# A 32-batch graph-attention kernel: the hardware loop over pairs of batches written out, all waits for constants

## The chip, the cores and the metric

The kernel runs on one core of one Trainium2 chip. The metric is the device time of one execution in microseconds. Before the change the median of three runs is 1394.42 us (1394.37 to 1395.95).

## What is computed

The reference takes 32 batches of 256 rows by 384 features, with one 256 x 256 boolean adjacency matrix per batch, and applies two residual layers:

```python
h = jnp.maximum(_layernorm(x, axis=-1), 0.0)
x = x + _L0_gnn_ref(h, Wq, bq, Wk, bk, Wv, bv, Wf, bf, adj)      # 6 heads of 64, masked softmax attention
h = jnp.maximum(_layernorm(x, axis=-1), 0.0)
x = x + _L1_gnn_ref(h, adj, W, b, w_src, w_dst, H_w, H_b)        # 12 heads of 32, graph attention, ELU, gate
```

In the second layer the score of a pair of rows is a sum of a source term and a destination term through a leaky ReLU, masked, and put through a softmax; the result passes an ELU and is mixed with the input by a sigmoid gate. The batches don't depend on one another.

## The kernel before, in words

All weights are loaded once and kept as two 16-bit parts each (three products make one), so the steady work is per batch. A batch is 256 rows in two tiles of 128 partitions; two to five batches are in flight at a time. Work is cut in steps (LN_T0, Q, K, QK, PT0, PV0, ...), each of which has a part on one or more engines.

The order of the steps is written out by hand for each engine, in ORDERS (L72 to L105). An entry such as `B GATE 0` names a phase, a step and an index; LAG (L64) says how far the phase's batch lies behind the iteration's number, so one iteration does phase L of batch n+2, P of n+1, A of n, B of n-1, C of n-2. `walk` (L382) goes through the iterations -2 to NB+2. Iterations -2 to 3 and 30 to 34 are written out ("straight code" in what follows). Iterations 4 to 29 are a hardware loop: `eng.Fori(0, LOOP)` (L394) with LOOP = 13 turns and two iterations in its body. Each engine has a loop of its own, with its own branch at the end of the body; so there are 12 jumps back per engine, and the thirteenth branch falls through.

The engines meet through semaphores that only count up. Count and Jobs (L121, L162) work out the value that a wait needs. In straight code it is a constant. In the loop it is an expression of the loop's register (`_value`, L145), which register instructions on the waiting engine compute before the wait. Where a wait comes several to an instruction, `ready` (L357) moves the value to one of three registers ahead of time, and the functions then wait for `s_pool_const` to reach 8, which has long been so, before the wait itself. DMA addresses of x, adj and the output are indexed with the loop register on the SP queue (`of_batch`, L424).

The steps that the texts below speak of:

- PE: `to_rows` (L501, products that make rows: V, OUT0, HEADS, GATE), `to_columns` (L515, Q and K), `transpose_probs` (L574), `qk` (L550), `pv1` (L637), `ln_t0` and `ln_t1` (L489). One iteration of PE's order begins with `C PT1 9, A QK 0, B GATE 0` and ends with `B PT1 8, B PV1 1`.
- DVE: `leaky1` (L986 and L993, steps SCORES1). The order ends with `B SCORES1 9` and begins with `C SCORES1 10`, so the end of the body lies between these two.
- ACT: `exp1` (L755) and `pt1` (L763). The order ends with `B EXP1 9` and begins with `C PT1 8, C EXP1 10`.
- POOL: `norm1` (L1115) and `norm0` (L1099); SP: the loads of x and adj and the store.

`qk` for index 0 writes a PSUM bank that SCORES1 11 reads and writes, and so waits for it (L544).

Of the kernel before, what the change touches and what calls it, by code (L numbers as in the profile page):

```python
# [50 lines left out]
YB = 3  # L51
# [56 lines left out]
class Batch:  # L108


    def __init__(self, ref, reg=None):
        self.ref, self.reg = ref, reg

    def back(self, k):
        return Batch(self.ref - k, self.reg)

    def value(self):
        return self.ref if self.reg is None else self.reg * 2 + self.ref


class Count:  # L121


    def __init__(self, n_batch, engine, per_step, unit=1):
        self.order, self.per_step, self.unit, self.n = ORDERS[engine], per_step, unit, n_batch
        self.starts = {-2: 0}
        for it in range(-2, n_batch + 3):
            self.starts[it + 1] = self.starts[it] + sum(per_step[s] for ph, s, _ in self.order if self._on(ph, it, s))
        self.per = self.starts[5] - self.starts[4]

# [13 lines left out]

    def _value(self, batch, n):  # L145
        v = n * self.unit
        return v if batch.reg is None else batch.reg * (2 * self.per * self.unit) + v

    def before(self, batch, step, idx=0, less=0):

        return self._value(batch, self._ahead(batch, step, idx) - less)

# [4 lines left out]
    def after(self, batch, step, idx=0, k=None):  # L157

        return self._value(batch, self._ahead(batch, step, idx) + (self.per_step[step] if k is None else k))


class Jobs(Count):  # L162
# [3 lines left out]
    def __init__(self, n_batch):  # L166
        super().__init__(n_batch, "PE", JOBS)
        assert 2 * self.per % self.BANKS == 0

# [7 lines left out]
    def before(self, batch, step, idx=0):  # L177

        v = self._ahead(batch, step, idx) // self.BANKS
        return v if batch.reg is None else batch.reg * (2 * self.per // self.BANKS) + v  # L180

# [4 lines left out]
def build(nc, x, adj, w_all, bq, bk, bv, bf, gat_b, w_src, w_dst, gate_b, out):  # L186
    NB = x.shape[0]
    LOOP = (NB - 6) // 2
    assert NB % 2 == 0 and LOOP >= 1

# [5 lines left out]
    with ExitStack() as ctx:  # L196
# [159 lines left out]

        def ready(eng, value):  # L357

            if isinstance(value, int):
                return value
            if eng.engine not in count_regs:
                count_regs[eng.engine] = [eng.alloc_register(f"count{i}_{eng.engine.name}") for i in range(3)]
            regs = count_regs[eng.engine]
            regs.append(regs.pop(0))
            eng.reg_mov(regs[-1], value)
            return regs[-1]

        count_regs = {}  # L370

        def loaded(b):

            v = 16 * (b.ref // 2 + 1)
            return v if b.reg is None else b.reg * 16 + v

# [5 lines left out]
        def walk(eng, order, parts, after={}):  # L382


            def iteration(it, reg=None):
                for phase, step, idx in order:
                    b = Batch(it - LAG[phase], reg)
                    if step in parts and 0 <= b.ref < NB:
                        parts[step](b, b.ref % 2, idx)
            for n in range(-2, 4):  # L390
                iteration(n)
                if n in after:
                    after[n]()
            with eng.Fori(0, LOOP) as j:  # L394
                iteration(4, j)
                iteration(5, j)
            for n in range(NB - 2, NB + 3):
                iteration(n)

# [4 lines left out]
        def _(sp):  # L404
# [18 lines left out]

            def of_batch(view, b, rows):  # L424
                return view[b.value()] if b.reg is None else view[bass.ds(b.value(), 1)].rearrange(rows)

            def load_x(b, par, _):
                x_b = of_batch(x_v, b, "a p t h -> (a p) t h")
                if b.ref >= 2:
                    sp.wait_ge(s_norm0, n_norm0.after(b.back(2), "NORM0"))  # L430
                    sp.wait_ge(s_xc, n_xc.after(b.back(2), "RES_ROW"))
                sp.dma_start(xb[par][:], x_b).then_inc(s_x[par], 16)

            def load_adj(b, par, _):
                adj_b = of_batch(adj_v, b, "a p t m -> (a p) t m")
                if b.ref >= 2:
                    used = ready(sp, n_mask1.after(b.back(2), "MASK1"))
                    sp.wait_ge(s_pool_const, 8)
                    sp.wait_ge(s_mask1, used)
                sp.dma_start(adj_raw[par][:], adj_b).then_inc(s_adj[par], 16)  # L440

            def store(b, par, _):
                out_b = of_batch(out_v, b, "a p t h -> (a p) t h")
                sp.wait_ge(s_sum, n_sum.after(b, "OUT_SUM"))
# [7 lines left out]
        def _(pe):  # L452
# [166 lines left out]
            def dst_t(b, par, _):  # L619
                bank, made, taken, _ = job(b, "DST_T")  # L620
                parts, free = ready(pe, n_sd.after(b, "SCORE_SUM")), ready(pe, n_job.before(b, "DST_T"))
                pe.wait_ge(s_pool_const, 8)
                pe.wait_ge(s_sd, parts)
# [157 lines left out]
        def _(dve):  # L781
# [49 lines left out]
            def gate_bias():  # L831

                own(V.tensor_scalar(gate_b_row[:], gate_b_row[:], wscale[:, WG:WG + 1], XS, ALU.mult, ALU.mult))
                for k in range(3):
# [13 lines left out]
            def aggregate(b, k, step, idx=0):  # L848
                written = ready(dve, n_bn.after(b, step, idx))
                dve.wait_ge(s_pool_const, 8)  # L850
                dve.wait_ge(s_bn, written)
# [57 lines left out]
            def scores0(b, par, u):  # L909
                masks = ready(dve, n_mask0.after(b, "MASK0"))  # L910
                scores = ready(dve, n_qk.after(b, "QK", u // 2))
                used = ready(dve, n_e0.before(b, "EXP0", u, YB - 1))
                dve.wait_ge(s_pool_const, 8)
                if u == 0:
# [54 lines left out]
            def leaky1(b, par, u):  # L969
# [19 lines left out]
                for hh in range(2):  # L989
                    written = ready(dve, n_lk.after(b, "SCORES1", u, hh + 1))  # L990
                    dve.wait_ge(s_pool_const, 8)
                    dve.wait_ge(s_lk, written)
# [41 lines left out]
        def _(pool):  # L1034
# [24 lines left out]
            def make_mask0(b, par, _):  # L1059
                here = ready(pool, loaded(b))  # L1060
                read = ready(pool, n_y0.after(b.back(1), "SCORES0", 5)) if b.ref >= 1 else None
                pool.wait_ge(s_pool_const, 8)
                pool.wait_ge(s_adj[par], here)
# [4 lines left out]
            def make_mask1(b, par, _):  # L1068
                here = ready(pool, loaded(b))
                read = ready(pool, n_y1.after(b.back(1), "SCORES1", 11)) if b.ref >= 1 else None  # L1070
                pool.wait_ge(s_pool_const, 8)
                pool.wait_ge(s_adj[par], here)
# [4 lines left out]
            def make_rstd(k, step, sstep):  # L1077
                def part(b, par, _):

                    here = ready(pool, n_mv.after(b, sstep))  # L1080
                    pool.wait_ge(s_pool_const, 8)
                    pool.wait_ge(s_mv, here)
# [6 lines left out]
            def norm0(b, par, _):  # L1089
                here = ready(pool, n_rstd.after(b, "RSTD0"))  # L1090
                if b.ref >= 1:
                    _, made, _, value = job(b.back(1), "LN_T0", 1)
                    used = ready(pool, value)
                pool.wait_ge(s_pool_const, 8)
                pool.wait_ge(s_rstd, here)
# [7 lines left out]
            def norm1(b, par, _):  # L1103
                here = ready(pool, n_rstd.after(b, "RSTD1"))
                if b.ref >= 1:
                    _, made, _, value = job(b.back(1), "LN_T1", 1)
                    used = ready(pool, value)
                    kept = ready(pool, n_hskip.after(b.back(1), "SKIP_H"))
                pool.wait_ge(s_pool_const, 8)
                pool.wait_ge(s_rstd, here)  # L1110
# [8 lines left out]
            def normp0(b, par, u):  # L1119
                here = ready(pool, n_np0.after(b, "NORMP0", u))  # L1120
                pool.wait_ge(s_pool_const, 8)
                pool.wait_ge(s_rec0, here)
# [31 lines left out]
            def gates(b, par, _):  # L1154

                jobs_ = [job(b, "GATE", t) for t in range(NT)]
                tanh = [ready(pool, value) for _, _, _, value in jobs_]
                used = ready(pool, n_fin.after(b.back(2), "FINISH", 1)) if b.ref >= 2 else None
                pool.wait_ge(s_pool_const, 8)
                for (_, _, taken, _), value in zip(jobs_, tanh):  # L1160
# [68 lines left out]
```

## Time and profile before

| | |
|---|---|
| median of 3 runs | 1394.42 us |
| profiled execution, device time | 1395.05 us |
| its span | 1393.1 us |
| PE (TensorE matmul) busy | 93% of the span |
| ACT, DVE, POOL busy | 91%, 88%, 65% |
| mean granted TensorE clock | 0.978 |

The device time is 1.95 us more than the span: what lies before the first and after the last recorded instruction. A "pause" is idle time in front of an instruction; in a timeline it stands in square brackets, with the instruction that ended it. "Issue" is time in which an engine waits for nothing that the profile shows. PEld is the weight load of TensorE.

### The profile page before, as it was taken

The numbers are of one execution on the slowest core, as the hardware profiler recorded it, in microseconds if no ns is written. First come the engines' busy times: TensorE is split into PE (matmuls) and PEld (weight loads), VectorE is DVE, ScalarE is ACT, GpSimd is POOL, SyncE is SP. The second block draws the span as 40 slices with busy tenths as digits, with TensorE's granted clock in tenths as the row PEclk, the third lists the DMA queues.
The fourth block names the chain that finished last, engine by engine and source line by source line (L and its number), as shares of the span: only waits on it lengthen the run. The fifth ranks groups of instructions, "written<-read, shape, count | busy, mean of one in ns | idle before, by whom it ended". The sixth has DMA issues, their size and how long they took to land.

```text
span 1393.1 us, 39297 instructions
## 1 busy us (share of the span) xinstructions
PE 1302.0 (93%) x10502; PEld 908.3 (65%) x10502; DVE 1221.0 (88%) x4457; ACT 1261.6 (91%) x3731; POOL 904.1 (65%) x1106
## 2 busy tenths in 40 slices
PE   2889999999999999999999999999999999999974
PEld 1567667766666776666677676767667666666642
DVE  3569999989898998989899898999989899999875
ACT  4469999989999999999999999999999999999975
POOL 3357777657766666777766676766667676567743
PEclk8899999999999999999999999999999999999986
DMA  5000000000000000000000000000000000000000
GB/s 151 13 14 15 26 13 27 27 26 14 26 25 13 25 25 26 14 26 15 23 25 25 15 25 26 12 26 25 25 15 25 25 14 26 25 25 3 13 13 24
DMA packets 29845, 33.28 MB, mean 24 GB/s; under 512 B 10464, under 2 KB 29664, under 8 KB 29664
## 3 DMA queue, kind: packets, MB, share of 16 engines
q1 hardware_dynamic: 29664, 31.62, 7.4%
q14 instruction: 159, 1.30, 0.3%
q8 instruction: 22, 0.36, 0.1%
HBM read 19.03 MB, written 12.58 MB: 23 GB/s over the span
## 4 chain that ended last, share of the span: by engine, by line
PE 48%; issue 15%; ACT 15%; DVE 14%; POOL 3%; DVEq 2%; DMA 1%; ACTq 0%; SPq 0%; POOLq 0%
PE job L501 14%; PE pt L574 10%; PE unit L550 7%; PE job L637 5%; DVE unit L986 4%; ACT p L755 4%; PE job L515 4%; ACT p L712 3%; PE job L489 3%; DVE y L993 3%; PE job L592 2%; ACT o1m L773 1%; ACT c L724 1%; DVE bn L868 1%; POOL xn L1115 1%
## 5 line engine op out<-in xcount | busy, mean ns | idle before, releaser
L755 ACT ACTIVATE p<-y,min 128x256 f32<-128x256 f32 x768 | 394.5, 537 | 10.2 <-DVE min L993 10.1
L986 DVE SCALAR_TENSOR_TENSOR unit<-unit,s,dst 128x256 f32<-128x256 f32 x768 | 336.6, 484 | 37.8 <-ACT p L755 33.6
L574 PE MATMUL pt<-ident,p 128*128 128x128 f32 x2304 | 356.6, 280 | 9.4 <-ACT p L755 5.6
L574 PEld LDWEIGHTS pt<-ident,p 128*128 128x128 f32 x2304 | 266.0, 142 | 84.5 <-issue 45.3
L501 PE MATMUL job<-w,h 128*128 128x384 f16 x1728 | 303.9, 328 | 0.9 <-DVE h L884 0.6
L993 DVE CUSTOM_DVE_ANT_0 y<-unit,mask 128x256 f32<-128x256 f32 x768 | 291.6, 417 | 0.3 <-issue 0.2
L1124 POOL TENSOR_SCALAR p<-p,rec 128x256 f32<-128x256 f32 x384 | 188.3, 506 | 116.1 <-DVE rec L927 111.5
L501 PEld LDWEIGHTS job<-w,h 128*128 128x128 f16 x1728 | 167.2, 98 | 107.9 <-DVE h L884 5.6
L763 ACT ACTIVATE pT<-pt 128x512 f32<-128x512 f32 x384 | 230.2, 621 | 7.4 <-issue 6.6
L712 ACT ACTIVATE p<-y,min 128x256 f32<-128x256 f32 x384 | 191.0, 503 | 37.5 <-PE pt L574 24.6
L515 PE MATMUL job<-h,w 128*128 128x256 f16 x1728 | 216.6, 274 | 1.4 <-DVE h L884 1.4
L920 DVE CUSTOM_DVE_ANT_0 y<-unit,mask 128x256 f32<-128x256 f32 x384 | 146.4, 421 | 45.4 <-PE unit L550 42.9
L515 PEld LDWEIGHTS job<-h,w 128*128 128x128 f16 x1728 | 169.6, 99 | 21.7 <-issue 1.8
L755 ACT ACTIVATION_READ_ACCUMULATOR p<-y,min 128x1 f32 x768 | 175.8, 229 | 0.0
L1185 POOL TENSOR_TENSOR y<-y,xskip 128x768 f32<-128x768 f32 x32 | 58.1, 1816 | 174.1 <-DVE y L1024 174.1
L550 PE MATMUL unit<-kT,qT 64*128 64x256 f32 x768 | 111.2, 409 | 28.1 <-DVE unit L986 23.5
L719 ACT ACTIVATE pT<-pt 128x512 f32<-128x512 f32 x192 | 111.3, 600 | 12.2 <-PE pt L574 12.1
L743 ACT ACTIVATE dst<-unit 128x512 f32<-128x512 f32 x192 | 118.3, 617 | 2.6 <-PE unit L565 1.7
L501 PE MATMUL job<-w,c 128*128 128x384 f16 x576 | 104.2, 327 | 1.0 <-DVE c L932 1.0
L637 PE MATMUL job<-pT,hv 128*32 128x256 f32 x1536 | 103.7, 388 | 0.7 <-ACT pT L763 0.7
L550 PEld LDWEIGHTS unit<-kT,qT 64*128 64x128 f32 x768 | 67.3, 189 | 52.7 <-DVE unit L986 26.3
L592 PE MATMUL job<-pT,vv 128*64 128x256 f32 x768 | 99.5, 395 | 0.0
(109 smaller groups left out, 2234.0 us busy)
## 6 DMA issues: line engine op xcount, KB each, us to landing
xb<-in_x_dram SPq DMA_DIRECT2D x32, 384.0 KB, 3.3
out_dram<-y SPq DMA_DIRECT2D x32, 384.0 KB, 2.5
pT<-in_w_all_dram SPq DMA_DIRECT2D x4, 576.0 KB, 10.4
adj_raw<-in_adj_dram SPq DMA_DIRECT2D x32, 64.0 KB, 1.9
prod<-in_w_all_dram SPq DMA_DIRECT2D x1, 576.0 KB, 5.0
p<-in_w_all_dram SPq DMA_DIRECT2D x1, 576.0 KB, 11.0
out_row<-in_bf_dram SPq DMA_DIRECT2D x1, 192.0 KB, 4.1
gate_b_row<-in_gate_b_dram SPq DMA_DIRECT2D x1, 192.0 KB, 6.2
```

What stands on the lines that cost most here:

```text
L501: last = mm(bank[:, 0:H], rows[:, i, c, t * P:(t + 1) * P], w16[:, w, j, c, :], start=n == 0, stop=(c, i, j) == (NC - 1, *TERMS[-1]))
L515: last = mm(bank[:, 0:T], w16[:, w, i, c, p * P:(p + 1) * P], h16[0][:, j, c, :], start=n == 0, stop=n == 3 * NC - 1)
L550: last = mm(unit_ps[(2 * p + hh) % 3][:, qt * T:(qt + 1) * T], qT[par][r, p, qt * P:(qt + 1) * P], kT[par][r, p, :], start=True, stop=True)
L574: last = nc.tensor.transpose(pt_ps[u % 2][:, (2 * hh + kt) * P:(2 * hh + kt + 1) * P], probs[:, u % 3, hh, kt * P:(kt + 1) * P], ident[:])
L637: last = mm(bank[D1 * q:D1 * (q + 1), 0:T], hv[par][:, kt, h * D1:(h + 1) * D1], pT1[:, g % 2, q, kt, :], start=kt == 0, stop=kt == NT - 1 ...
L712: last = op(p0[:, u % 3, hh, :], y0[:, u % YB, hh, :], ACT.Exp, bias=min0[:, u, hh:hh + 1], scale=-1.0, accum_out=sum0[:, u, hh:hh + 1])
L755: last = op(p1[:, u % 3, hh, :], y1[:, u % YB, hh, :], ACT.Exp, bias=min1[:, u, hh:hh + 1], scale=-1.0, accum_out=sum1[:, t, h:h + 1])
L763: op(pT1[:, g % 2, q_:q_ + 2, :, t * P:(t + 1) * P], pt_ps[u % 2][:].rearrange("p (h k q) -> p h k q", h=2, k=NT), ACT.Copy).then_inc(s_pT, 1)
L920: last = V.tensor_tensor_reduce(y0[:, u % YB, qt, :], unit_ps[u % 3][:, qt * T:(qt + 1) * T], mask0[:, qt, :], 1.0, 3.0e38, ALU.add, ALU.m ...
L986: V.scalar_tensor_tensor(leaky[:, hh * T:(hh + 1) * T], bank[:, hh * T:(hh + 1) * T], s8[par][:, t, h:h + 1], dst5[:, c % 2, hh, :], ALU.a ...
L993: last = V.tensor_tensor_reduce(y1[:, u % YB, hh, :], leaky[:, hh * T:(hh + 1) * T], mask1[:, t, :], 1.0, 3.0e38, ALU.add, ALU.min, min1[: ...
L1124: last = G.tensor_scalar(p0[:, u % 3, hh, :], p0[:, u % 3, hh, :], rec0[:, u, hh:hh + 1], 1.0, ALU.mult, ALU.mult)
```

## The change

The loop is gone: `walk` writes out all iterations in the same order. A batch has no register, every count is a constant, `ready` and the extra waits for `s_pool_const` are gone (one stands in the bias code of DVE and one ahead of POOL's walk), and the SP queue's addresses are constants.

```diff
-            def iteration(it, reg=None):
+            for n in range(-2, NB + 3):
                 for phase, step, idx in order:
-                    b = Batch(it - LAG[phase], reg)
+                    b = Batch(n - LAG[phase])
                     if step in parts and 0 <= b.ref < NB:
                         parts[step](b, b.ref % 2, idx)
-            for n in range(-2, 4):
-                iteration(n)
                 if n in after:
                     after[n]()
-            with eng.Fori(0, LOOP) as j:
-                iteration(4, j)
-                iteration(5, j)
-            for n in range(NB - 2, NB + 3):
-                iteration(n)
...
-    def _value(self, batch, n):
-        v = n * self.unit
-        return v if batch.reg is None else batch.reg * (2 * self.per * self.unit) + v
-
     def before(self, batch, step, idx=0, less=0):
 
-        return self._value(batch, self._ahead(batch, step, idx) - less)
+        return (self._ahead(batch, step, idx) - less) * self.unit
...
-                x_b = of_batch(x_v, b, "a p t h -> (a p) t h")
+                x_b = x_v[b.ref]
...
             def dst_t(b, par, _):
                 bank, made, taken, _ = job(b, "DST_T")
-                parts, free = ready(pe, n_sd.after(b, "SCORE_SUM")), ready(pe, n_job.before(b, "DST_T"))
-                pe.wait_ge(s_pool_const, 8)
+                parts, free = n_sd.after(b, "SCORE_SUM"), n_job.before(b, "DST_T")
                 pe.wait_ge(s_sd, parts)
                 pe.wait_ge(taken, free)
...
             def gate_bias():
 
+                dve.wait_ge(s_pool_const, 8)
...
                 for hh in range(2):
-                    written = ready(dve, n_lk.after(b, "SCORES1", u, hh + 1))
-                    dve.wait_ge(s_pool_const, 8)
+                    written = n_lk.after(b, "SCORES1", u, hh + 1)
                     dve.wait_ge(s_lk, written)
...
+            pool.wait_ge(s_pool_const, 8)
             walk(pool, ORDERS["POOL"],
```

The other places where `ready` and the wait for `s_pool_const` stood (SCORES0, the aggregates, the masks, RSTD, NORM0, NORM1, NORMP0, GATES, LOAD_ADJ) are changed in the same way.

## Rows read from the trace of the kernel before

**Rows 1.** The page: the span, and PE's busy time.

```profile
span 1393.1 us, 39297 instructions
PE 1302.0 (93%) x10502; PEld 908.3 (65%) x10502; DVE 1221.0 (88%) x4457; ACT 1261.6 (91%) x3731; POOL 904.1 (65%) x1106
```

**Rows 2.** Chain that ended last, whole span: start us, us, what (its longest pieces).

```profile
153.73 2.99 PE job L501 x18
...
193.61 2.99 PE job L501 x18
233.66 2.99 PE job L501 x18
...
317.27 2.99 PE job L501 x18
...
399.45 2.99 PE job L501 x18
...
481.36 2.99 PE job L501 x18
...
1218.95 2.99 PE job L501 x18
...
1258.83 2.99 PE job L501 x18
...
1298.70 2.99 PE job L501 x18
```

**Rows 3.** The chain in 135 to 175 us, straight code: shares by line.

```profile
by line: PE job L501 29.7%; PE pt L574 21.8%; PE job L515 15.3%; PE unit L550 8.0%; PE job L637 7.5%; PE job L592 7.3%; PE unit L565 3.8%; PE job L489 3.6%; PE job L645 1.6%; PE job L497 1.1%; PE job L627 0.5%
```

**Rows 4.** Stretches of PE: start:end us, length, PE busy, PEclk, DMA, GB/s.

```profile
135.00:175.00 40.00, 40.00 (x331) 1.00 0.08 23
...
282.60:286.10 3.50, 3.50 (x15) 0.51 0.00 0
...
440.00:522.00 82.00, 79.97 (x659) 1.00 0.07 22
```

**Rows 5.** Timeline of all engines around the second jump back.

```profile
360.29 0.09 DVE L993 DVE_READ_ACCUMULATOR2_ANT min<- 128x1 f32 x1
...
362.31 0.56 ACT L755 ACTIVATE p<-y,min 128x256 f32<-128x256 f32 x1
...
363.38 0.88 DVE L986 SCALAR_TENSOR_TENSOR unit<-unit,s,dst 128x256 f32<-128x256 f32 x2 [3.01 <-ACT p L755]
363.68 0.60 ACT L763 ACTIVATE pT<-pt 128x512 f32<-128x512 f32 x1 [0.72 <-issue]
...
365.92 0.49 PE L550 MATMUL unit<-kT,qT 64*128 64x256 f32 x2 [2.17 <-DVE unit L986]
```

**Rows 6.** The chain in 358 to 367 us, around the same jump: two pieces.

```profile
360.37 2.70 issue
363.08 0.06 DVEq L394
```

**Rows 7.** Timeline of DVE where the thirteenth branch falls through.

```profile
1261.97 0.08 DVE L993 DVE_READ_ACCUMULATOR2_ANT min<- 128x1 f32 x1
1262.18 0.88 DVE L986 SCALAR_TENSOR_TENSOR unit<-unit,s,dst 128x256 f32<-128x256 f32 x2
```

**Rows 8.** Waits in 215 to 255 us (an even iteration of the loop).

```profile
PEld job L489 <- POOL xn L1115: 0.4, 1, 0.4
```

**Rows 9.** DMA queues in 90 to 265 us (packets, MB, share), and one issue.

```profile
q8 instruction: 12, 0.20, 0.5%
q14 instruction: 14, 0.11, 0.2%
...
xb<-in_x_dram SPq DMA_DIRECT2D x5, 384.0 KB, 3.5
```

**Rows 10.** DMA queues in 300 to 1262 us (the turns after the first), and one issue.

```profile
q1 hardware_dynamic: 19040, 19.99, 6.6%
q14 instruction: 126, 1.03, 0.3%
...
xb<-in_x_dram SPq DMA_DIRECT2D x23, 384.0 KB, 3.3
```

**Rows 11.** Whole span, the SP queue's waits: us, times, longest.

```profile
SPq L439 <- POOL mask L1075: 727.5, 30, 38.5
```

**Rows 12.** The page: the granted TensorE clock in 40 slices.

```profile
PEclk8899999999999999999999999999999999999986
```

More of the change, by code:

```diff
@@ L108, with __init__ @@
 class Batch:
-    def __init__(self, ref, reg=None):
-        self.ref, self.reg = ref, reg
+    def __init__(self, ref):
+        self.ref = ref
     def back(self, k):
-        return Batch(self.ref - k, self.reg)
-    def value(self):
-        return self.ref if self.reg is None else self.reg * 2 + self.ref
+        return Batch(self.ref - k)
 class Count:
@@ L128, in __init__ @@
             self.starts[it + 1] = self.starts[it] + sum(per_step[s] for ph, s, _ in self.order if self._on(ph, it, s))
-        self.per = self.starts[5] - self.starts[4]
     def _on(self, phase, it, step):
@@ L157, in after @@
     def after(self, batch, step, idx=0, k=None):
-        return self._value(batch, self._ahead(batch, step, idx) + (self.per_step[step] if k is None else k))
+        return (self._ahead(batch, step, idx) + (self.per_step[step] if k is None else k)) * self.unit
 class Jobs(Count):
@@ L167, in __init__ @@
         super().__init__(n_batch, "PE", JOBS)
-        assert 2 * self.per % self.BANKS == 0
     def bank(self, batch, step, idx):
@@ L177, in before @@
     def before(self, batch, step, idx=0):
-        v = self._ahead(batch, step, idx) // self.BANKS
-        return v if batch.reg is None else batch.reg * (2 * self.per // self.BANKS) + v
+        return self._ahead(batch, step, idx) // self.BANKS
     def after(self, batch, step, idx=0):
@@ L187, in build @@
     NB = x.shape[0]
-    LOOP = (NB - 6) // 2
-    assert NB % 2 == 0 and LOOP >= 1
     x_v = x.rearrange("b (t p) h -> b p t h", p=P)
@@ L355, in build @@
         s_out, n_out = sem("s_stored"), Count(NB, "SP", {"STORE": 1}, 16)
[L357 to L370, printed above, removed]
         def loaded(b):
-            v = 16 * (b.ref // 2 + 1)
-            return v if b.reg is None else b.reg * 16 + v
+            return 16 * (b.ref // 2 + 1)
         def job(b, step, idx=0):
@@ L422, in _ @@
             load_weight(WK)
-            def of_batch(view, b, rows):
-                return view[b.value()] if b.reg is None else view[bass.ds(b.value(), 1)].rearrange(rows)
             def load_x(b, par, _):
-                x_b = of_batch(x_v, b, "a p t h -> (a p) t h")
+                x_b = x_v[b.ref]
                 if b.ref >= 2:
@@ L434, in load_adj @@
             def load_adj(b, par, _):
-                adj_b = of_batch(adj_v, b, "a p t m -> (a p) t m")
+                adj_b = adj_v[b.ref]
                 if b.ref >= 2:
-                    used = ready(sp, n_mask1.after(b.back(2), "MASK1"))
-                    sp.wait_ge(s_pool_const, 8)
+                    used = n_mask1.after(b.back(2), "MASK1")
                     sp.wait_ge(s_mask1, used)
@@ L442, in store @@
             def store(b, par, _):
-                out_b = of_batch(out_v, b, "a p t h -> (a p) t h")
+                out_b = out_v[b.ref]
                 sp.wait_ge(s_sum, n_sum.after(b, "OUT_SUM"))
@@ L848, in aggregate @@
             def aggregate(b, k, step, idx=0):
-                written = ready(dve, n_bn.after(b, step, idx))
-                dve.wait_ge(s_pool_const, 8)
+                written = n_bn.after(b, step, idx)
                 dve.wait_ge(s_bn, written)
@@ L909, in scores0 @@
             def scores0(b, par, u):
[L910 to L913, printed above, removed]
+                masks = n_mask0.after(b, "MASK0")
+                scores = n_qk.after(b, "QK", u // 2)
+                used = n_e0.before(b, "EXP0", u, YB - 1)
                 if u == 0:
@@ L989, in leaky1 @@
                 for hh in range(2):
-                    written = ready(dve, n_lk.after(b, "SCORES1", u, hh + 1))
-                    dve.wait_ge(s_pool_const, 8)
+                    written = n_lk.after(b, "SCORES1", u, hh + 1)
                     dve.wait_ge(s_lk, written)
@@ L1059, in make_mask0 @@
             def make_mask0(b, par, _):
-                here = ready(pool, loaded(b))
-                read = ready(pool, n_y0.after(b.back(1), "SCORES0", 5)) if b.ref >= 1 else None
-                pool.wait_ge(s_pool_const, 8)
+                here = loaded(b)
+                read = n_y0.after(b.back(1), "SCORES0", 5) if b.ref >= 1 else None
                 pool.wait_ge(s_adj[par], here)
@@ L1068, in make_mask1 @@
             def make_mask1(b, par, _):
-                here = ready(pool, loaded(b))
-                read = ready(pool, n_y1.after(b.back(1), "SCORES1", 11)) if b.ref >= 1 else None
-                pool.wait_ge(s_pool_const, 8)
+                here = loaded(b)
+                read = n_y1.after(b.back(1), "SCORES1", 11) if b.ref >= 1 else None
                 pool.wait_ge(s_adj[par], here)
@@ L1078, in part @@
                 def part(b, par, _):
-                    here = ready(pool, n_mv.after(b, sstep))
-                    pool.wait_ge(s_pool_const, 8)
+                    here = n_mv.after(b, sstep)
                     pool.wait_ge(s_mv, here)
@@ L1089, in norm0 @@
             def norm0(b, par, _):
-                here = ready(pool, n_rstd.after(b, "RSTD0"))
+                here = n_rstd.after(b, "RSTD0")
                 if b.ref >= 1:
                     _, made, _, value = job(b.back(1), "LN_T0", 1)
-                    used = ready(pool, value)
-                pool.wait_ge(s_pool_const, 8)
+                    used = value
                 pool.wait_ge(s_rstd, here)
@@ L1103, in norm1 @@
             def norm1(b, par, _):
-                here = ready(pool, n_rstd.after(b, "RSTD1"))
+                here = n_rstd.after(b, "RSTD1")
                 if b.ref >= 1:
                     _, made, _, value = job(b.back(1), "LN_T1", 1)
-                    used = ready(pool, value)
-                    kept = ready(pool, n_hskip.after(b.back(1), "SKIP_H"))
-                pool.wait_ge(s_pool_const, 8)
+                    used = value
+                    kept = n_hskip.after(b.back(1), "SKIP_H")
                 pool.wait_ge(s_rstd, here)
@@ L1119, in normp0 @@
             def normp0(b, par, u):
-                here = ready(pool, n_np0.after(b, "NORMP0", u))
-                pool.wait_ge(s_pool_const, 8)
+                here = n_np0.after(b, "NORMP0", u)
                 pool.wait_ge(s_rec0, here)
@@ L1156, in gates @@
                 jobs_ = [job(b, "GATE", t) for t in range(NT)]
-                tanh = [ready(pool, value) for _, _, _, value in jobs_]
-                used = ready(pool, n_fin.after(b.back(2), "FINISH", 1)) if b.ref >= 2 else None
-                pool.wait_ge(s_pool_const, 8)
+                tanh = [value for _, _, _, value in jobs_]
+                used = n_fin.after(b.back(2), "FINISH", 1) if b.ref >= 2 else None
                 for (_, _, taken, _), value in zip(jobs_, tanh):
```

## The prediction

> **What bounds the kernel now.** I read the page first for the span and the shares: PE is busy for 93% of 1393.1 us [rows 1], so it is the first suspect, but an average over straight code and loop can't say what a jump costs. So the second view is the chain that ended last, and in it one piece that comes back once per batch, the run of 18 products of L501 [rows 2]. Its starts are a clock for the batches. In straight code and in the first half of a turn they lie 39.88 us apart (153.73 to 193.61), and after the loop 39.87 (1258.83 to 1298.70). Inside the loop two batches take 81.91 us (399.45 to 481.36), where two of 39.87 would take 79.74. The loop is slower by 2.17 us per turn, and the place is to be found.
>
> In straight code the chain from 135 to 175 us consists of PE instructions alone, its shares by line adding up to 100% [rows 3], and PE is busy for 40.00 of 40.00 us [rows 4]. There no wait and no other engine decides anything: 39.87 us is PE's own work for a batch. In the loop PE is busy for 79.97 of 82.00 us [rows 4], so it idles about 2.03 us in a turn. The timeline shows where: DVE ends the last instruction of its loop body at 360.38, its next, the first of the body, starts at 363.38 after a pause of 3.01 us; and PE stands idle for 2.17 us before L550 at 365.92, released by that DVE step [rows 5]. The pause is put down to an ACT activation of L755, but DVE's next step, SCORES1 10, needs only EXP1 7 (YB is 3), and the activation at 362.31 is EXP1 9; the chain calls the same stretch 2.70 us of issue [rows 6]. What lies there in the program is the branch. ACT has a pause of issue as well, 0.72 us before its first instruction of the body [rows 5], short because its queue still held work. At the thirteenth branch, which falls through to straight code, DVE goes from 1261.97 plus 0.08 to 1262.18, a gap of 0.13 us [rows 7]. So it is the jump back that costs, not the register work ahead of it nor the last counts of a turn.
>
> **The change part by part.** All sums are against the profiled execution: span 1393.1 us, device time 1395.05 us, which is 0.63 us above the median of the runs.
>
> *The jumps.* 12 per engine are removed. In the chain's clock: from 193.61 to 233.66 is 40.05 us, 0.18 over 39.87; the next two batches (to 317.27) take 83.61, 3.87 over; the two after (to 399.45) 82.18, 2.44 over; the two after 81.91, 2.17 over; from 481.36 to 1218.95 are 18 batches in 737.59 us, 19.93 over, 2.21 a turn; then 39.88 and 39.87, 0.01 over [rows 2]. From 153.73 to 1298.70 there are 28 batches in 1144.97 us; 28 x 39.87 is 1116.36; the excess is **28.61 us**. Ahead of and behind this stretch all is straight code before and after, so I cost that at nothing.
>
> *The clock.* The first jump's 3.87 us is 1.70 above a plain one's. From 282.6 to 286.1 us, right behind PE's pause, the granted clock is 0.51, which is the 1.2 GHz level, and 3.50 us at half speed lose 1.7 us [rows 4]. That is in the 28.61. Later pauses of the same size cost no clock [rows 12], so this one could come back elsewhere; without a pause there is less to cause it. I take it as saved and put 1.7 us in the range.
>
> *Register instructions and moved values.* They go on all engines. In the straight stretch, where the waits are constants, PE has no pause to lose [rows 3, 4]. In the loop the even iterations have 0.18 us more: there the weight load of L489 waits 0.4 us for POOL's normalised rows [rows 8], while odd ones don't pay. This is inside the 28.61. Bounds: nothing, or 13 x 0.18 = 2.3 us that could stay if it is not the registers. I take it as saved, since straight iterations on both sides of the loop lack it.
>
> *The waits for s_pool_const.* Straight code has them today and still runs at 39.87 with PE alone in the chain [rows 3]; the cover is PE's own work. Removing them can't shorten a chain that they aren't in. Below that bound nothing; above it, small idle moments that the modelled ends of matmuls hide, which I put at up to 0.1 us a batch, 3 us, for the range alone. The added waits on DVE (ahead of the gate bias) and POOL (ahead of its walk) wait for what POOL has made long before, or had to wait for anyway in its first step; behind them stand DVE's setup and POOL's steps, which PE's start-up waits for, but no later than today.
>
> *SP.* The addresses become constants. SP waits 727.5 us in 30 waits for a mask before a load of adj [rows 11], so its own instructions are far from the end. Loads of x land in 3.5 us in straight code and 3.3 in the loop [rows 9, 10]: nothing.
>
> *Instruction fetch.* This is what the change adds. PE fetched 12 packets of instructions on q8 in 175 us of straight code and first turn, 2.7 a batch [rows 9], and none from 300 to 1262 us [rows 10]: its body stays in its memory. Written out, PE fetches through 24 more batches, 66 packets. The other engines fetched 14 packets on q14 in that 175 us, and 126 in the 962 us of loop, where they reload the body every turn [rows 9, 10]; for them nothing is new except that the fetches come in order. The cost for PE: the 39.87 us of straight code was had with these very packets under way and PE never idle [rows 3, 4, 9]. I cost it at nothing; what hides it is that a packet lasts PE 175 / 12, some 15 us. If the cover were gone it is the rival below.
>
> A rule of the Trainium skill speaks against the trace here. The page "Advanced Engine Details and Errata", section ISA Cache, gives the instruction memory as only two lines of 16 KB. By it PE would reload its body each turn too and the change would add no traffic; the absence of q8 in the loop disagrees.
>
> Sum: 1395.05 - 28.6 = 1366.4 for an execution like the profiled one; against the median, 1394.42 - 28.6 = 1365.8. I say **1365.9 us**, 2.0% less.
>
> **The rivals.** *The pause moves instead of going (1391).* A straight DVE program also passes on to new instruction packets. If the pause were due to that and not to the jump, it would come back somewhere in every two batches, and only branch and register work would be saved: 12 branches at 0.06 us as DVE's queue shows one [rows 6], and 13 x 0.18 for the even iterations, 3.0 us together. Against it: DVE's gap of 0.13 us where the branch falls through [rows 7], and no idle PE in straight code [rows 4]. Chance 0.03. The page "Advanced Engine Details and Errata" of the Trainium skill, section Control Flow Timing, gives a compare-and-branch about 108 ns: by that alone the 12 jumps are worth 1.3 us and the time would be 1393.1. The pause of 3.01 us at the jump disagrees.
>
> *PE starves for instructions (slower, 1413).* Place: PE's queue, at each of the 66 new packets. An engine that waits for code with work still queued paused for 0.72 us (ACT), one without for 3.01 us (DVE) [rows 5]. PE is the full engine, so I take the former: 66 x 0.72 is 47.5 us, less 28.6 is 18.9 slower. It turns the sign from 28.6 / 66 = 0.43 us a packet. For it: fetches of all engines meet the 384 KB loads for longer. Against it: 12 packets passed with five loads of x under way [rows 9] while PE was busy for 40.00 of 40.00 us. Chance 0.03.
>
> *Half the gain (1382).* One packet in three shows in this way: 22 x 0.72 = 15.8 us of the 28.6 are given back. The same rows speak against it. Chance 0.05.
>
> *The clock gives way without the small pauses.* Straight code ran at 1.00 through 135 to 215 us, and to 282.6; a stretch of 3.5 us at half costs 1.7, so 17 of them would eat the gain. Nothing of this in rows 12. Chance 0.01, with the slower side.
>
> That the change does not do what it says has no room: order and waits are the same by the diff, and the loop is gone from the text.
>
> **How the numbers follow.** Forecast 0.88, half the gain 0.05, moved pause 0.03, slower 0.04. The time is the forecast's. The range takes the terms' bounds: down 3 us for hidden idle moments and 1 for run-to-run spread, 1362; up 2.3 (even iterations) and 1.7 (a clock dip elsewhere) and 0.9 of spread, 1371. Faster by over 0.2% (2.8 us, about what a measurement of this kernel can tell from no change) 0.93, within 0.2% 0.03, slower 0.04.
>
> **What would show it.** Right: the L501 pieces 39.87 us apart from start to end, DVE without 3 us pauses, PE's share of the span near 95%, q8 packets all the way at 2.7 a batch, granted clock 1.00 from 60 to 1290 us. Wrong: issue time on PE near q8 packets; batches of 40.05 that remain every second time would cost 2.3 us; a period above 40.97 us in the 26 batches would turn the sign.

## The result, and the profile after

The changed kernel takes **1360.42 us** (median of 4 runs, 1360.17 to 1361.86) against 1394.87 us before (4 runs); the ratio is 0.9754, 95% interval [0.9737, 0.9771]. That is 34.5 us or 2.5% less, where 28.6 us were forecast. Sign and main cause were right; the time lies 1.6 us below the stated range of 1362.0 to 1371.0, so more than one term of the sum was off. Two of all executions that follow were slow ones (1417.64 us of the kernel before, 3315.52 us of e2), and the ratios leave them out.

The profiled execution took 1360.17 us, 34.88 less than the one of before. Its page, where the loss of the 5787 instructions is in the first line (register, branch and wait instructions; the busy ones are as many as before [rows 1]):

```profile
span 1358.3 us, 33510 instructions
PE 1293.0 (95%) x10502; PEld 905.9 (67%) x10502; DVE 1213.5 (89%) x4457; ACT 1252.5 (92%) x3731; POOL 903.3 (66%) x1106
```

The chain that ended last in the changed kernel (start us, us, what; the products of `to_rows` are now L462) gives the same clock for the batches as [rows 2]:

```profile
152.75 2.92 PE job L462 x18
...
192.50 2.93 PE job L462 x18
...
232.25 2.93 PE job L462 x18
...
311.74 2.93 PE job L462 x18
...
1225.96 2.93 PE job L462 x18
...
1265.71 2.93 PE job L462 x18
```

From 152.75 to 1265.71 are again 28 batches, now in 1112.96 us; 39.75 us each, with no step of two. Before it was 1144.97 us. So 32.01 of the 34.88 us lie here. Of these, 28.61 are the excess over 39.87 us that the prediction counted; the other 3.40 us are 0.12 us a batch, because the batches are also faster than straight code was before. Of the remaining 2.87 us, 0.98 lie ahead of the first mark and 1.81 behind the last. Behind the last mark PE is busy for 65.89 us at a mean granted clock of 0.81 before, and for 64.08 us at 0.84 now; why was not tested.

The stretches of PE, as [rows 4], and the whole written-out part behind them:

```profile
440.00:522.00 82.00, 82.00 (x676) 1.00 0.08 22
...
57.00:1320.00 1263.00, 1251.37 (x10271) 1.00 0.07 22
```

The 2 us of idle PE in every two batches are gone. The page's queues show where the fetches went, as [rows 9, 10]:

```profile
q8 instruction: 86, 1.41, 0.4%
q14 instruction: 89, 0.73, 0.2%
```

PE fetches 86 packets where the whole kernel before fetched 22, 64 more (66 had been worked out). The others fetch 89 where they fetched 159. In e1 below, which differs from the kernel before by the loop alone, they fetch 98: in the loop they fetched their bodies again and again.

### The profile page after: what moved, and what is told of

Same layout as the page of the kernel before. It is cut to its first block, busy times and chain, and to the rows that moved or that the text cites. A ratio compares the mean times of both kernels' runs of the same rounds, so it can differ in the third digit from the quotient of the medians.

```text
span 1358.3 us, 33510 instructions
## 1 busy us (share of the span) xinstructions
PE 1293.0 (95%) x10502; PEld 905.9 (67%) x10502; DVE 1213.5 (89%) x4457; ACT 1252.5 (92%) x3731; POOL 903.3 (66%) x1106
## 4 chain that ended last, share of the span: by engine, by line
PE 89%; ACT 2%; DVE 1%; issue 1%; POOL 1%; POOLq 0%; DVEq 0%; ACTq 0%
PE job L462 26%; PE pt L535 20%; PE job L476 13%; PE unit L511 7%; PE job L597 7%; PE job L553 7%; PE unit L526 3%; PE job L450 3%; PE job L605 2%; PE job L458 1%; ACT p L715 1%; PE job L587 1%; DVE unit L945 0%; POOL prod L1098 0%; ACT pT L723 0%
## 5 line engine op out<-in xcount | busy, mean ns | idle before, releaser
L462 PE MATMUL job<-w,h 128*128 128x384 f16 x1728 | 301.8, 326 | 0.7 <-DVE h L844 0.6
L462 PEld LDWEIGHTS job<-w,h 128*128 128x128 f16 x1728 | 166.5, 98 | 104.7 <-issue 0.8
L715 ACT ACTIVATION_READ_ACCUMULATOR p<-y,min 128x1 f32 x768 | 179.9, 234 | 0.0
L679 ACT ACTIVATE pT<-pt 128x512 f32<-128x512 f32 x192 | 111.5, 602 | 11.8 <-PE pt L535 11.7
L462 PE MATMUL job<-w,c 128*128 128x384 f16 x576 | 104.2, 327 | 1.0 <-DVE c L891 1.0
L1130 POOL TENSOR_TENSOR o<-o,gat_b_row 128x768 f32<-128x768 f32 x32 | 58.3, 1823 | 52.9 <-DVE o L968 52.9
```

Of the source, the lines that this page charges most:

```text
L462: last = mm(bank[:, 0:H], rows[:, i, c, t * P:(t + 1) * P], w16[:, w, j, c, :], start=n == 0, stop=(c, i, j) == (NC - 1, *TERMS[-1]))
L715: last = op(p1[:, u % 3, hh, :], y1[:, u % YB, hh, :], ACT.Exp, bias=min1[:, u, hh:hh + 1], scale=-1.0, accum_out=sum1[:, t, h:h + 1])
```

## The experiments

Each kernel was timed against the kernel before on the same chip; there the latter took 1394.28 us (for e1 to e4), 1393.28 us (e5 to e8) and 1393.70 us (e9 to e12). The ratios are against these and compare best. The last column is twice the usual period of a batch in the profiled execution, single longer batches left out.

| run | us | ratio to before, 95% interval | two batches, steady |
|---|---|---|---|
| before | 1394.87 | | 81.9 |
| changed | 1360.42 | 0.9754 [0.9737, 0.9771] | 79.5 |
| e1 straight, waits kept | 1367.95 | 0.9810 [0.9797, 0.9823] | 79.7 |
| e3 one turn, no registers in effect | 1367.65 | 0.9805 [0.9791, 0.9820] | 79.7 |
| e4 only DVE straight | 1366.78 | 0.9805 [0.9790, 0.9819] | 79.7 |
| e5 only DVE loops | 1394.63 | 1.0008 [0.9998, 1.0017] | 81.9 |
| e12 six turns | 1379.08 | 0.9893 [0.9877, 0.9908] | 81.9, then 79.7 |
| e2 one wait back, norm1 | 1361.71 | 0.9761 [0.9748, 0.9774] | 79.5 |
| e6 aggregate waits back | 1360.91 | 0.9765 [0.9752, 0.9779] | 79.5 |
| e7 RSTD waits back | 1362.75 | 0.9780 [0.9767, 0.9793] | 79.5 |
| e8 SCORES1 waits back | 1360.80 | 0.9768 [0.9755, 0.9781] | 79.5 |
| e9 three kinds back | 1367.19 | 0.9809 [0.9795, 0.9822] | 79.7 |
| e10 all but those kept | 1361.66 | 0.9768 [0.9755, 0.9782] | 79.5 |

### Is it the jump, the registers or the waits?

**e1**, the kernel before without the loop, all waits for `s_pool_const` kept:

```diff
-            with eng.Fori(0, LOOP) as j:
-                iteration(4, j)
-                iteration(5, j)
-            for n in range(NB - 2, NB + 3):
+            for n in range(4, NB + 3):
                 iteration(n)
```

> The loop is written out but every wait for s_pool_const stays. Theory A (the forecast's sum was right for the loop, and what it missed is the removal of those waits, which shortens the way DVE, POOL, PE ahead of LN_T1): 28.6 us off, about 1366, the L501 pieces 39.87 us apart. Theory B (the missing 5 us come from the missing loop too, say from less work in the sequencers, or from chance at the start): about 1360 to 1361, pieces 39.75 apart as in the changed kernel.

Measured: 1367.95 us, and a plain period of 39.86 us. The loop alone is worth 26.3 us at the medians, near the 28.6 of the sum. Not every batch kept to 39.86: some took 0.1 to 0.4 us more, 1.5 us in 28 batches, which I have not traced to a cause. The profiled execution also has a stretch at half clock near 91 us, worth about 1.7 us, that the kernel before and the changed kernel have not (see the last experiments); so the waits are not worth all of the 7.5 us between e1 and the changed kernel.

**e3** was meant to work out every count from a register, in a body that is run once:

```diff
-            with eng.Fori(0, LOOP) as j:
-                iteration(4, j)
-                iteration(5, j)
+            with eng.Fori(0, 1) as j:
+                for n in range(4, NB - 2):
+                    iteration(n, j)
```

> Iterations 4 to 29 in the body of a loop of one turn: every count is still worked out from a register, but nothing jumps back. Theory jump: the jumps are 12 x 2.0 us and the clock dip 1.7, so about 1394.5 - 26 = 1368 to 1369, with every or every second batch at 40.05 us. Rival (register instructions cost most of the 2.17 us a turn): 1385 or more, periods above 40.5.

Measured: 1367.65 us, the time of e1, plain periods of 39.86. But this run doesn't test the registers. Its page counts 34740 instructions where e1 has 34725 and the kernel before 39297: 15 more, three for each of five engines. With a single turn the counts must have become constants when the program was built, so e3 is a second e1. What the register instructions cost is read from e4 and e5 below.

**e12** keeps 6 of the 13 turns:

> The kernel before with 6 turns in place of 13, the rest written out: 5 jumps instead of 12. If the cost is per jump: 7 x 2.17 = 15.2 us less, 1378 to 1380, and the rest at 39.86 to 39.9 a batch. If the loop's cost is in entering it, or in its first turns: less than 8 us.

```diff
-            with eng.Fori(0, LOOP) as j:
+            with eng.Fori(0, 6) as j:
...
-            for n in range(NB - 2, NB + 3):
+            for n in range(16, NB + 3):
```

Measured: 1379.08 us, 14.6 less than before (1393.7 in that comparison) for 7 turns fewer, 2.1 us each. The cost comes with each turn, not with entering the loop.

### Whose jump is it?

`walk` is called once per engine, so each engine can loop or not by itself. **e4** writes out DVE alone, **e5** lets DVE alone loop:

```diff
+            if order is not ORDERS["DVE"]:      # e5: if order is ORDERS["DVE"]:
                 with eng.Fori(0, LOOP) as j:
                     iteration(4, j)
                     iteration(5, j)
+            else:
+                for n in range(4, NB - 2):
+                    iteration(n)
```

> Only DVE's program is written out; PE, ACT, POOL and SP keep their loops and jumps, and the waits for s_pool_const stay. Theory DVE (its reload after the jump is the pause that PE feels, the other engines have queued work or slack): nearly all of the 28.6 us go, about 1367 to 1371. Rival (each engine's jump costs on its own, ACT's 0.72 us of issue comes next, or PE's own jump is felt): half or more stays, 1380 or more.

> The counterpart of the run in which only DVE was written out: only DVE keeps its loop and its 12 jumps, all other engines are written out, the waits for s_pool_const stay. Theory DVE: the whole loss is back, 1392 to 1395, with two batches in about 81.9 us. Rival (it needs the loops of PE or ACT as well): below 1385.

Measured: 1366.78 and 1394.63 us. With DVE written out the other four engines may loop for nothing; with DVE looping nothing is gained by writing out the other four. The chain of e5 shows the old picture (start us, us, what); the issue at 277.26 is the first jump:

```profile
194.16 2.99 PE job L505 x18
234.18 2.99 PE job L505 x18
277.26 2.46 issue
...
399.87 2.99 PE job L505 x18
...
481.77 2.99 PE job L505 x18
524.85 2.43 issue
```

and the timeline of e5, at the end of DVE's body, the old pause with all other engines in straight code:

```profile
445.65 0.88 DVE L990 SCALAR_TENSOR_TENSOR unit<-unit,s,dst 128x256 f32<-128x256 f32 x2 [2.70 <-ACT p L759]
...
448.28 1.10 PE L554 MATMUL unit<-kT,qT 64*128 64x256 f32 x7 [1.95 <-DVE unit L990]
```

In e4 the same marks run through without steps, though PE, ACT, POOL and SP jump back 12 times: 1117.31 us for 28 batches, 39.90 each.

```profile
154.44 2.99 PE job L505 x18
...
194.29 2.99 PE job L505 x18
...
234.17 2.99 PE job L505 x18
...
473.56 2.99 PE job L505 x18
...
1271.75 2.99 PE job L505 x18
```

These two runs also price the register instructions. e4 keeps them on all engines but DVE (37580 instructions on its page, 2855 more than e1) and is no slower than e1, so there they cost nothing that shows. On DVE they do: the batch from 193.61 to 233.66 us of the kernel before, 0.18 us too long [rows 2], lies ahead of the first jump. It is 40.02 us in e5, where only DVE has registers (194.16 to 234.18), and 39.88 us in e4, where DVE has none (194.29 to 234.17); e3, which enters a loop but has no registers, has 39.86 us there. So about 0.15 us of each turn belongs to DVE's register instructions and not to the jump, at least in the first turn; in later ones this batch and the jump fall together and can't be told apart.

### Why does DVE's jump cost 3 us and ACT's nothing?

**e11** adds, behind DVE's last step, loops of four turns over bodies of 100 to 1000 waits that are fulfilled already, each followed by the body once in straight code:

```diff
+            V.memset(marks[:, 0:1], 0.0)
+            for k, size in enumerate((100, 200, 400, 600, 1000)):
+                with dve.Fori(0, 4):
+                    for _ in range(size):
+                        dve.wait_ge(s_pool_const, 8)
+                V.memset(marks[:, 2 * k + 1:2 * k + 2], 0.0)
+                for _ in range(size):
+                    dve.wait_ge(s_pool_const, 8)
+                V.memset(marks[:, 2 * k + 2:2 * k + 3], 0.0)
```

> The changed kernel, and behind the last step of DVE loops of four turns over 100, 200, 400, 600 and 1000 waits that are fulfilled already, each followed by as many waits in straight code, with a small memset between the stretches as a mark. If the jump costs because the body is reloaded: four turns over 100 and 200 take four times the straight stretch plus some tenths of a us, while from 400 or 600 up each jump back adds 2 to 3 us (6 to 9 us in a loop). If it costs by itself, 100 pays it too.

It was executed once. The timeline of DVE (the idle time before a mark is the stretch of waits; L995 ends a loop, L998 the straight copy):

```profile
1373.49 0.06 DVE L995 MEMSET marks<- 128x1 f32 x1 [19.69 <-issue]
1378.39 0.06 DVE L998 MEMSET marks<- 128x1 f32 x1 [4.84 <-issue]
1419.66 0.06 DVE L995 MEMSET marks<- 128x1 f32 x1 [41.21 <-issue]
1429.82 0.06 DVE L998 MEMSET marks<- 128x1 f32 x1 [10.10 <-issue]
1510.85 0.06 DVE L995 MEMSET marks<- 128x1 f32 x1 [80.97 <-issue]
1530.81 0.06 DVE L998 MEMSET marks<- 128x1 f32 x1 [19.90 <-issue]
1662.71 0.06 DVE L995 MEMSET marks<- 128x1 f32 x1 [131.84 <-issue]
1692.80 0.06 DVE L998 MEMSET marks<- 128x1 f32 x1 [30.02 <-issue]
1903.33 0.06 DVE L995 MEMSET marks<- 128x1 f32 x1 [210.48 <-issue]
1953.68 0.06 DVE L998 MEMSET marks<- 128x1 f32 x1 [50.29 <-issue]
```

Four straight copies of 400 would take 79.6 us, the loop took 80.97, 1.4 more for three jumps and the loop's entry. Four of 600 would take 120.1, the loop took 131.84: 11.8 more, 3.9 a jump. For 1000 it is 9.3 more, 3.1 a jump; for 100 and 200 it is 0.3 and 0.8 in all. So over such waits, and without any register, a jump of DVE is nearly free up to 400 instructions and costs 3 to 4 us from 600 on. The queue of instruction packets agrees: first the loop over 400 (1430 to 1510 us), then that over 600 (1531 to 1662 us).

```profile
q14 instruction: 2, 0.02, 0.0%
...
q14 instruction: 17, 0.14, 0.4%
```

In the kernel before, the trace records 508 DVE instructions in one turn (442.2 to 524.1 us), 376 of ACT and 143 of POOL. By e11 alone ACT would be free because its body is short. The packets speak against this. From 300 to 1200 us the engines other than PE fetch 88 packets in e4, where DVE is written out and ACT, POOL and SP loop, and 68 in e1, where nothing loops. And behind ACT's jump in e4 (437.3 to 441 us) there are packets, as there are behind DVE's in e5 (442.5 to 446.5 us); e4 first:

```profile
q14 instruction: 2, 0.02, 1.6%
...
q14 instruction: 3, 0.02, 1.6%
```

In the same place of e4 ACT pauses 0.53 us:

```profile
440.01 0.60 ACT L767 ACTIVATE pT<-pt 128x512 f32<-128x512 f32 x1 [0.53 <-issue]
```

So ACT probably fetches its body again as well, though it has fewer than 400 instructions, and its jump is cheap because it still has work queued. This is argued and not shown: POOL jumps at nearly the same time, and the queue doesn't tell whose packets it carries. Shown is only that ACT's pause does not reach PE. PE has 1459 instructions in that turn (656 matmuls, as many weight loads, and 147 waits and register instructions) and isn't reloaded [rows 10], so its limit must be another; it was not tried.

The page "Runtime: NRT & Kernel Launch" of the Trainium skill, section Instruction fetch mechanics, states that a jump to a block outside the fetched window stalls for a fetch, and "Advanced Engine Details and Errata" of the Trainium skill, section ISA Cache, that the window is 32 KB (2 lines of 256 instructions), 128 KB on TensorE. The 512 instructions lie between the 400 and 600 of e11, and the larger size for TensorE agrees with the missing q8 packets; in the prediction I set only the page's "two lines" against that row and not its TensorE size. The size alone doesn't settle this case, for DVE's body of 508 recorded instructions pays, and ACT's of 376 may well be fetched again. "Advanced Engine Details and Errata" of the Trainium skill, section Control Flow Timing, gives about 108 ns for a compare-and-branch. The small bodies agree (0.3 us for three jumps over 100), the large ones don't.

### Which waits give the other 0.12 us a batch?

The timelines show the way from the statistics of the second layer norm to its transposes. Before:

```profile
146.94 1.01 DVE L868 BATCH_NORM_STATS2 bn<-x 128x6 f32<-128x384 f32 x2
148.05 0.25 DVE L853 BATCH_NORM_AGGREGATE mv<-bn 128x2 f32<-128x6 f32 x2
148.45 0.19 POOL L1083 TENSOR_SCALAR nmean<-mv 128x2 f32<-128x2 f32 x1 [1.92 <-DVE mv L853]
149.85 1.31 POOL L1115 TENSOR_SCALAR xn<-x,nmean,rstd 128x384 f32<-128x384 f32 x2 [0.17 <-POOL rstd L1086]
151.22 0.55 PE L489 MATMUL job<-ident,xn 128*128 128x128 f32 x3
```

and in the changed kernel:

```profile
146.02 1.00 DVE L828 BATCH_NORM_STATS2 bn<-x 128x6 f32<-128x384 f32 x2
147.06 0.25 DVE L813 BATCH_NORM_AGGREGATE mv<-bn 128x2 f32<-128x6 f32 x2
147.39 0.19 POOL L1038 TENSOR_SCALAR nmean<-mv 128x2 f32<-128x2 f32 x1 [1.77 <-DVE mv L813]
148.73 1.31 POOL L1068 TENSOR_SCALAR xn<-x,nmean,rstd 128x384 f32<-128x384 f32 x2
150.24 0.38 PE L450 MATMUL job<-ident,xn 128*128 128x128 f32 x2
```

Before, NORM1 starts 1.90 us after BN_STATS ends (147.95 to 149.85), now 1.71 us (147.02 to 148.73): 0.19 us less in three links (aggregate, RSTD, NORM1), in each of which a wait for `s_pool_const` stood ahead of the real one. And before, PE's transposes start 0.06 us after NORM1 ends at 151.16; in the changed kernel 0.20 us after it ends at 150.04. So before PE was held up here, and now its first transpose has 0.14 us to spare.

How often this reaches PE stands in the waits of the whole span (us, times, longest). DVE makes `h` from these transposes, and the weight loads of `to_rows` wait for it. In the kernel before, the changed one, e9 and e10 (the last two are explained below):

```profile
PEld job L501 <- DVE h L884: 5.6, 30, 0.7
```
```profile
PEld job L462 <- DVE h L844: 0.5, 1, 0.5
```
```profile
PEld job L462 <- DVE h L845: 5.4, 30, 0.5
```
```profile
PEld job L498 <- DVE h L880: 1.6, 3, 1.2
```

The kernels with a period of 39.85 us or more have this wait 30 times (e1 and e4 too), those with 39.75 us at most 5 times.

**e2**, **e6**, **e7** and **e8** put one kind of these waits back into the changed kernel; e2's edit:

```diff
                     kept = n_hskip.after(b.back(1), "SKIP_H")
+                pool.wait_ge(s_pool_const, 8)
                 pool.wait_ge(s_rstd, here)
```

> The changed kernel with a single wait for s_pool_const put back, in POOL's norm1 ahead of its wait for s_rstd. In the kernel before, POOL pauses 0.17 us there and in the changed one not. Theory A1 (this one wait is the 0.12 us a batch): period 39.87 us, 3.8 us slower than the changed kernel, 1364. Theory A2 (it is one of the waits on DVE or in POOL's RSTD1): period 39.75, 1360 to 1361.

> The changed kernel with the wait for s_pool_const back in DVE's aggregate, twice a batch, between bn_stats and the wait for s_bn. If this is where the 0.12 us a batch came from: period 39.87 and 1364 to 1366. If not: 39.75 and 1360 to 1361.

> The changed kernel with the wait for s_pool_const back in POOL's RSTD0 and RSTD1 only, ahead of the wait for the mean and variance. If this is where the 0.12 us a batch came from: period 39.87 and 1364 to 1366. I expect 39.75, since POOL stands idle for 1.8 us there and has the extra wait behind it long before.

> The changed kernel with the 24 waits a batch for s_pool_const back in DVE's SCORES1 only. If DVE is late because its sequencer has these instructions to work through: period 39.8 to 39.87, and single longer batches as in the straight kernel with all waits kept (40.1 to 40.3), 1363 to 1367. If not: 39.75 throughout.

The edits of the others, e6 in `aggregate`, e7 in `make_rstd`, e8 in SCORES1:

```diff
                 written = n_bn.after(b, step, idx)
+                dve.wait_ge(s_pool_const, 8)
...
                     here = n_mv.after(b, sstep)
+                    pool.wait_ge(s_pool_const, 8)
...
                     written = n_lk.after(b, "SCORES1", u, hh + 1)
+                    dve.wait_ge(s_pool_const, 8)
```

Each of them leaves the plain period at 39.73 to 39.75 us, and e8 does so with 24 more instructions a batch on DVE (five single batches are longer there by 0.1 to 0.2 us). Taken alone, e2's expectation A1 and e6's first one fell. After them I took the three links together:

> The changed kernel with the waits for s_pool_const back in DVE's aggregates, POOL's RSTD and norm1 together; each of them alone left the period at 39.75. In the changed kernel the way from the end of BN_STATS to NORM1 is 0.19 us shorter than before, by three steps of about 0.06, and the transposes of LN_T1 start 0.13 us later after NORM1 than they could. Theory sum: one step fits in that 0.13 us, three don't; the period goes to 39.80 to 39.87, 1362 to 1365. Rival (it is the waits on DVE or PE elsewhere, or all of them together): 39.75, 1361.

> The complement: the straight kernel with all waits for s_pool_const except those three kinds. Theory sum: the period is 39.75, with single longer batches if these come from DVE's additional instructions; 1361 to 1364. Rival: 39.86 and 1366 to 1368 as with all waits kept.

e9 has the three edits of e2, e6 and e7 at once; e10 is e1 with the opposite edit:

```diff
                 written = ready(dve, n_bn.after(b, step, idx))
-                dve.wait_ge(s_pool_const, 8)
...
                     here = ready(pool, n_mv.after(b, sstep))
-                    pool.wait_ge(s_pool_const, 8)
...
                     kept = ready(pool, n_hskip.after(b.back(1), "SKIP_H"))
-                pool.wait_ge(s_pool_const, 8)
```

Measured: e9 1367.19 us with a plain period of 39.85, e10 1361.66 us with 39.75. Each link is worth about 0.06 us: one step is hidden, three are not. The sizes don't close with 0.14 us to spare, though, for 0.19 us of links would then show as 0.05 us a batch, and 0.10 us is measured. The 0.14 us hold for the first transpose only. Beside the changed kernel, e9's first transpose of a batch is 0.04 us late (429 to 431 us of the traces), but the ones behind it and the products that wait for `h` are 0.10 us late; so the time that hides the links is about 0.09 us. What one such wait takes also shows in e11, where 1000 of them in straight code on DVE take 50.29 us, 0.05 us each.

The expected time of e9 (1362 to 1365) was exceeded by 2.2 us although the period was as expected. A part of that is the clock. e9 and e1 have one stretch of half clock in their first batches that the changed kernel has not; the stretches of PE are (start:end, length, busy, PEclk), in the changed kernel and in e9:

```profile
89.00:94.00 5.00, 4.97 (x42) 1.00 0.37 95
```
```profile
89.00:94.00 5.00, 4.91 (x28) 0.66 0.33 95
```

At half clock for 3.4 us this is 1.7 us. It follows two pauses of PE of about 1 us that the changed kernel has there too. Of the other profiled executions, those of e3, e4, e5, e7 and e12 have it as well, and those of before, e2, e6, e8 and e10 not; e7 is the slowest of the kernels with the short period. Why it comes in some and not in others is open.

## Why the prediction was wrong, and where right

*The bound, and the jumps (28.61 us).* Right. PE is the bound, DVE's jump makes the pause that PE feels; the period is regular without it. Removing the loop alone gave 26.3 us (e1), and counted over the 28 batches, 1144.97 against 1117.59 us, 27.4 us; the term was 1.2 us too high on account of the single longer batches.

*The place.* Right in the main: without DVE's loop the loss is gone with all other loops kept (e4), and jumps over large bodies cost 3 to 4 us without any register (e11). The prediction left open whether ACT's pause counts; it doesn't (e4). Not all of it is the jump, see the registers.

*The clock.* As assumed: the half-clock stretch at 282.6 us is gone, and none comes between 57 and 1288 us. That such a stretch can also come at 90 us was not foreseen.

*Register instructions.* The 0.18 us in the even iterations was taken as saved, and it was. It belongs to DVE's register instructions, about 0.15 us of it by e5 against e4. That PE was held up there by way of POOL's rows fits the reading of [rows 8].

*The waits for s_pool_const: the step that failed.* The prediction said that removing them "can't shorten a chain that they aren't in", because the chain of straight code consisted of PE alone and PE was busy for 40.00 of 40.00 us, and it put at most 0.1 us a batch in the range. Measured: 0.12 us a batch, 3.4 us in 28 batches. Between e1 and e10 (the same kernel but for the three kinds of waits) the savings against their own kernel before differ by 5.7 us (26.3 and 32.0), of which about 1.7 us are the clock at 90 us in the profiled executions; that leaves 4.0 us, and 0.12 us in each of 32 batches is 3.8 us. Both views hide a short wait of PE, since the ends of matmuls are modelled: the products ahead of the transposes are drawn as lasting up to them. Two things showed it beforehand. L489 started 0.06 us behind NORM1's end, right behind what it needs. And PE's weight loads, which the chain doesn't show, waited for DVE's `h` 30 times, 0.2 us each and in straight code too. The row of 0.4 us for L489 [rows 8] named the very place, and was read as a matter of the loop.

*Ahead of and behind the 28 batches.* The prediction cost this at nothing, because all of it is straight code before and after. Measured: 0.98 and 1.81 us less. Of this about 0.5 us would be the same waits in the four batches outside; the rest is open. Both terms were needed to leave the range: the profiled execution is 6.3 us below the sum's 1366.4, which is 3.40 for the period, 2.79 here, and 0.08 outside the span.

*Instruction fetch, SP.* Right. 64 more packets for PE against 66, at no cost that shows: the period stays at 39.75 us with them.

*The rivals.* The moved pause fell by e1 (no pause in straight code); the starving PE by the period of 39.75 us and by PE busy throughout. The bound of 3 us for hidden idle moments, which set the lower end of the range, was taken without a row.

## What to carry to other kernels

A jump back can cost an engine the time until its program is there again: 3 us on DVE here with 508 instructions in the body, 3 to 4 us with 600 or 1000, at most 0.5 us with 400 plain waits. Count each engine's instructions in the body, waits and register instructions too, and see whether work is queued behind the jump. Here only DVE's loop mattered, and writing out its program alone (e4) gave all of the loop's loss back with the other programs still looping. A wait that is always fulfilled is not free if it stands ahead of a real wait in a chain of short steps between engines: each cost about 0.06 us, and three together outweighed the spare time, where one did not. "Busy 100%" of a PE with modelled ends proves no absence of waits: compare the start of each group with the end of what it needs, and read the waits of the weight loads. And compare the instruction counts of a variant before trusting it: e3 was to keep the register instructions and had none.

## What the runs showed that was not expected

A DVE jump over 400 plain waits or fewer costs at most 0.5 us, over 600 or 1000 it costs 3.1 to 3.9 us. Register arithmetic ahead of the waits on PE, ACT, POOL and SP through 26 batches cost nothing measurable (e4, 1366.78 us, against e1, 1367.95 us); on DVE it cost about 0.15 us in the first turn. One stretch of 3.4 us at half clock near 90 us comes in some kernels and not in others with nearly the same start (e1 and e9 have it, the changed kernel and e10 don't); by the granted clock it is worth about 1.7 us.
